# Two attentions inside one core's hybrid kernel: cycles of eight even units, mixed score phases, and another split of the query and key sums

## The reference

```python
x = x + attn_a(layernorm(x))   # heads of 8 -> latent 32, rope, q' = q_lat @ wqk.T + b, causal softmax over 256 keys
x = x + ffn(layernorm(x))      # logits = flat @ gate_w + gate_b, top 2 of 8 experts, gelu MLP 128 -> 512 -> 128
x = x + attn_b(layernorm(x))   # heads of 8, causal softmax(q k / sqrt(8)) v, out @ Wo.T + bo
x = x + ffn(layernorm(x))      # the same experts again
```

## Time and profile before

| | us |
|---|---|
| median of three runs | 1544.81 |
| the three runs | 1544.81, 1550.25, 1526.23 |
| the profiled execution | 1524.42 |
| its span, first to last instruction | 1520.8 |
| granted TensorE clock over the span | 0.818 |
| busy: TensorE, VectorE, ScalarE, GpSimd | 1175.3, 789.3, 655.4, 856.6 |

### The profile page before, as it was taken

The page is one execution under the profiler, slowest core; times in us unless marked ns, Lnnn a source line. Parts: engine busy times, 40 slices in busy tenths (PEclk is TensorE's granted clock), DMA queues, the critical chain, the costliest instruction groups (busy, mean ns, idle before and its releaser), DMA issues.

```text
span 1520.8 us, 31294 instructions
## 1 busy us (share of the span) xinstructions
PE 1175.3 (77%) x11163; PEld 907.0 (60%) x11164; DVE 789.3 (52%) x1878; ACT 655.4 (43%) x1214; POOL 856.6 (56%) x1173
## 2 busy tenths in 40 slices
PE   2699998989898889557999377888889837899600
PEld 2566666666666666447999244555556526899600
DVE  4555545454545544383554156666666647456322
ACT  0244445354444544203555344666667610455300
POOL 0456556565556654165552567887766518555276
PEclk8588869697978988657999677999999955999855
DMA  8000000000000000002223000000000000233222
GB/s 208 0 2 1 2 8 2 8 8 2 9 1 8 2 8 2 28 0 58 78 76 59 24 18 16 22 23 22 20 4 8 15 21 14 67 76 75 51 80 74
DMA packets 56245, 45.69 MB, mean 30 GB/s; under 512 B 13570, under 2 KB 48258, under 8 KB 56130
## 3 DMA queue, kind: packets, MB, share of 16 engines
q0 software_dynamic: 9088, 18.63, 5.6%
q1 hardware_dynamic: 39378, 22.44, 5.2%
q10 hardware_dynamic: 7664, 3.04, 0.9%
HBM read 27.57 MB, written 16.52 MB: 29 GB/s over the span
## 4 chain that ended last, share of the span: by engine, by line
PE 57%; DVE 15%; ACT 9%; POOL 7%; issue 6%; DMA 3%; another core or an unknown queue 1%; ACTq 1%; DVEq 1%; POOLq 0%
PE PS L1617 9%; PE PS L1331 5%; PE PS L1441 5%; POOL got L657 5%; PE PS L1333 4%; PE PS L1332 4%; PE PS L1382 4%; PE PS L1400 4%; ACT PT L1130 3%; PE PS L1429 3%; PE PS L1413 2%; DVE M L854 2%; PE PS L1426 2%; ACT xn L1116 2%; DMA b_cols<-in_L_ffn_b_dram 2%
## 5 line engine op out<-in xcount | busy, mean ns | idle before, releaser
L1130 ACT ACTIVATE PT<-PS 128x768 f32<-128x768 f32 x256 | 207.0, 809 | 307.0 <-PE PS L1451 224.7
L553 POOL TENSOR_SCALAR_AFFINE_SELECT PT<-PT 128x256 f32<-128x256 f32 x512 | 200.9, 416 | 202.0 <-ACT PT L1130 201.2
L853 DVE TENSOR_REDUCE M<-PS 128x4 f32<-128x512 f32 x128 | 88.7, 693 | 271.2 <-PE PS L1429 180.2
L686 POOL DMA_INDIRECT xg<-normed,source x156 | 150.0, 961 | 116.6 <-PE PS L1595 80.0
L657 POOL DMA_INDIRECT got<-expert_rows,slot_of x128 | 122.1, 954 | 80.6 <-DMA expert_rows<-y_rows 46.3
L1257 ACT ACTIVATE hid<-PS,b_cols 128x256 f32<-128x256 f32 x312 | 122.3, 475 | 96.4 <-PE PS L1333 74.4
L1617 PE MATMUL PS<-W,hid 128*128 x1248 | 156.1, 279 | 3.2 <-ACT hid L1257 2.7
L854 DVE TENSOR_REDUCE M<-PS 128x4 f32<-128x1024 f32 x128 | 155.6, 1216 | 0.0
L1617 PEld LDWEIGHTS PS<-W,hid 128*128 128x128 f32 x1248 | 149.4, 195 | 4.5 <-issue 4.5
L1382 PE MATMUL PS<-causal_b,ident_b 128*128 128x256 bf16 x512 | 112.0, 306 | 48.4 <-DVE q_aug L916 28.9
L1400 PE MATMUL PS<-PT,v_aug 128*32 128x256 f32 (+1 forms) x2048 | 124.8, 367 | 12.6 <-POOL PT L553 12.6
(11 more groups left out here) (263 smaller groups left out, 3061.7 us busy)
## 6 DMA issues: line engine op xcount, KB each, us to landing
expert_rows<-y_rows SPq DMA_DIRECT2D x78, 128.0 KB
normed<-xn SPq DMA_DIRECT2D x16, 256.0 KB, 2.3
xg<-normed,source POOLq DMA_INDIRECT x156
W<-in_L_ffn_w_dram SPq DMA_DIRECT2D x1, 2048.0 KB, 16.0
got<-expert_rows,slot_of POOLq DMA_INDIRECT x128, 2.5
out_dram<-X SPq DMA_DIRECT2D x8, 256.0 KB
b_rows<-in_L_ffn_b_dram SPq DMA_DIRECT2D x2, 512.0 KB, 3.7
X<-in_L_attn_a_x_dram ACTq DMA_DIRECT2D x2, 256.0 KB, 4.5
```

The source lines that it names most:

```text
L553: ins = nc.gpsimd.affine_select(out=diagonal, in_=diagonal, pattern=[[0, 2], [1, P]], compare_op=ALU.is_ge, fill=0.0, base=0, channel_mult ...
L686: nc.gpsimd.indirect_dma_start(out=xg[:, i % 4, b_, :], out_offset=None, in_=normed, in_offset=bass.IndirectOffsetOnAxis(ap=source[:, k:k ...
L1130: s.activation(PT[:, unit % 2, 2 * pair:2 * pair + 2, :], PS[:, 4:6, 0:3 * P], ACT.Exp).then_inc(m["exp_done"], 1)
```

## The change

In A the straight scores of the next unit and the turned scores of this one are issued together: `phase(unit, pair, unit + 1)` takes straight scores of two heads and turned scores of the other two, so four row bands are in use in each term, and there are two phases a unit. The maximum is taken in two halves (`pair_max`), one behind each phase. The lists are dealt out again: `second` (query2) in even units ahead of phase 0, `project` (a query or a key) between the phases in each unit, `close` (one step of another kind) after phase 1 in each unit. A chunk's gate comes one cycle later, normalizing is cut in halves or pairs of tiles, and the epilogue uses several banks.

In B the first scores stand behind prep, query 0 and key 0; the prologue has six steps instead of ten. Gathers and adds are one a unit after the first cycle, statistics are taken tile by tile, with buffers of their own for the gate. The query's sum is one VectorE operation from PSUM (bias and `minus` added, no `whole`), keys stay with GpSimd; `adds` places rows of the next chunk between the prologue's steps. SP's stores of the normalized chunks are written out instead of looped.

The core of the diff (deep indentation shortened by twelve):

```diff
@@ class Step, PlanA, Plan @@
     FIRST = [("prep", 0, 7), ("query", 0, 6), ("key", 0, 5), ("value", 0, 4), ("query", 1, 7), ("key", 1, 6), ("query2", 0, 5)]
-    LATE = [None, ("turn", 1, -1), None, ("prep", 0, 1), None, ("value", 0, 1), None, ("gate_t", 0, -1)]
-    EXTRA = [("gate", 0, -2), None, ("out_t", 0, -1), None, ("out", 0, -1), None, ("turn", 0, 0), None]
-    LAST = [("gate", 0, -1), ("turn", 1, 0), ("out_t", 0, 0), ("out", 0, 0), ("gate_t", 0, 0), ("gate", 0, 0)]
+    CLOSE = [("value", 0, 1), ("turn", 1, -1), ("gate_t", 0, -2), ("gate", 0, -2), ("out_t", 0, -1), ("out", 0, -1), ("prep", 0, 2), ("turn", 0, 0)]
+    FIRST_CLOSE = [None, None, ("prep", 0, 1), None, ("value", 0, 1), None, ("prep", 0, 2), ("turn", 0, 0)]
+    LAST = [("turn", 1, 0, 7), ("gate_t", 0, -1, 0), ("gate", 0, -1, 1), ("out_t", 0, 0, 2), ("out", 0, 0, 3), ("gate_t", 0, 0, 7), ("gate", 0, 0, 0)]
...
-    FIRST = [("prep", 0, 7), ("query", 0, 6), ("key", 0, 5), ("value", 0, 4), ("query", 1, 7), ("key", 1, 6),
- ("query", 2, 5), ("key", 2, 4), ("query", 3, 6), ("key", 3, 7)]
+    FIRST = [("prep", 0, 7), ("query", 0, 6), ("key", 0, 5), ("query", 1, 7), ("key", 1, 6), ("value", 0, 4)]
...
-    LATE = [("value", 0, 1), ("turn", 1, -1), ("out_t", 0, -1), ("out", 0, -1), ("prep", 0, 2), ("turn", 0, 0), ("gate_t", 0, -1), ("gate", 0, -1)]
+    LATE = [("turn", 0, -1), ("turn", 1, -1), ("value", 0, 1), ("gate_t", 0, -2), ("out_t", 0, -1), ("out", 0, -1), ("gate", 0, -2), ("prep", 0, 2)]
...
+    LAST = [("turn", 1, 0, 7), ("gate_t", 0, -1, 0), ("out_t", 0, 0, 1), ("gate", 0, -1, 2), ("out", 0, 0, 3), ("gate_t", 0, 0, 7), ("gate", 0, 0, 0)]
...
@@ gathers_at, adds_at @@
-    return (c + 3, range(2 * u - 4, 2 * u - 2)) if 2 <= u < 6 and c + 3 < NCH else None
+    return (c + 3, range(u, u + 1)) if c + 3 < NCH else None
...
+        return {0: (1, range(5, 8)), 2: (2, range(0, 4)), 4: (2, range(4, 8)), 6: (3, range(0, 4)), 7: (3, range(4, 6))}.get(u)
+    chunk, k = (c + 3, u - 2) if u >= 2 else (c + 2, u + 6)
+    return (chunk, range(k, k + 1)) if chunk < NCH else None
...
@@ GpSimd, attention_a and attention_b @@
-        early = plan.early[unit]
+        if unit and plan.project[unit - 1]:
+            end_rope(plan.project[unit - 1])
+        mask(m, unit, 0)
         if u % 2 == 0 and unit // 2 + 1 < NCH * G:
             key_low(unit // 2 + 1)
-        if early:
-            start_rope(early)
-        mask(m, unit, 0)
-        if early:
-            end_rope(early)
+        if plan.project[unit]:
+            start_rope(plan.project[unit])
         mask(m, unit, 1)
-        if unit + 1 < NCH * UNITS and normal_a(unit + 1):
...
+    def stack_keys(s):
+        pool.wait_ge(m["freed_act"], s.freed)
+        nc.gpsimd.tensor_tensor(ks[:, s.c % 2, s.g, :, :].rearrange("p b s -> p (b s)"), whole[:, 1, :],
+                                minus[:, 1, :].bitcast(F32), ALU.add).then_inc(m["keys_ready"], 1)
+    gather_results("1", 1, range(0, 3))
+    root(m, 1)
+    for s in plan.prologue:
+        if s.kind == "key":
+            stack_keys(s)
+    gather_results("1", 1, range(3, 2 * CT))
+    for unit in range(NCH * UNITS):
+        c, u = divmod(unit, UNITS)
+        if plan.early[unit] and plan.early[unit].kind == "key":
+            stack_keys(plan.early[unit])
+        mask(m, unit, 0)
+        if plan.late[unit] and plan.late[unit].kind == "key":
+            stack_keys(plan.late[unit])
+        mask(m, unit, 1)
+        if gathers_at(unit):
+            gather_results("1", *gathers_at(unit))
+        if root_at(unit):
+            root(m, *root_at(unit))
+        if u == 1:
...
@@ VectorE: closing, pair_max, attention_a, attention_b @@
+    elif s.kind == "query":
+        dve.wait_ge(m["queries_minus"], s.stacked)
+        v.scalar_tensor_tensor(qs[:, s.c % 2, s.g, :, :].rearrange("p b s -> p (b s)"), at, w["bias"][:, 0, s.g:s.g + 1],
+                               minus[:, 0, :].bitcast(F32), ALU.add, ALU.add).then_inc(m["freed_dve"], 1)
...
+def pair_max(m, unit, pair):
+    dve.wait_ge(m["s_ready"], 2 * unit + pair + 1)
+    banks, cols = slice(2 - 2 * pair, 4 - 2 * pair), slice((2 - 2 * pair) * L, (4 - 2 * pair) * L, L)
+    v.tensor_reduce(M[:, 0, cols], PS[:, banks, 0:P], AX, ALU.max, negate=True)
+    ins = v.tensor_reduce(M[:, 1, cols], PS[:, banks, P:3 * P], AX, ALU.max, negate=True)
+    if pair == 1:
+        ins.then_inc(m["max_ready"], 1)
...
-    row_max(m, 0, 0)
+    pair_max(m, 0, 0)
+    pair_max(m, 0, 1)
     for unit in range(NCH * UNITS):
         c, u = divmod(unit, UNITS)
         if unit + 1 < NCH * UNITS:
-            row_max(m, unit + 1, 0)
-        if plan.late[unit]:
-            closing(m, w, plan.late[unit], True)
-        if u % 2 == 0 and unit // 2 + 1 < NCH * G:
+            pair_max(m, unit + 1, 0)
+        if plan.second[unit]:
             query_low(unit // 2 + 1)
-        if plan.early[unit]:
-            swap(plan.early[unit])
-        if plan.extra[unit]:
-            closing(m, w, plan.extra[unit], True)
+        if unit + 1 < NCH * UNITS:
+            pair_max(m, unit + 1, 1)
+        if plan.close[unit]:
+            closing(m, w, plan.close[unit], True)
         if statistics_a(unit) is not None:
             if statistics_a(unit) < c:
                 dve.wait_ge(m["freed_dve"], plan.find("out", 0, c - 1).freed)
             statistics(m, statistics_a(unit))
+        if plan.project[unit]:
+            swap(plan.project[unit])
...
+    add_expert_rows("1", 1, range(0, 2), False)
+    adds = {("prep", 0): 2, ("query", 0): 3, ("key", 0): 4}
     for s in plan.prologue:
         closing(m, w, s, False)
-    row_max(m, 0, 3 * HD)
+        if (s.kind, s.g) in adds:
+            k = adds[s.kind, s.g]
+            add_expert_rows("1", 1, range(k, k + 1), False)
+        if (s.kind, s.g) == ("key", 0):
+            row_max(m, 0, 3 * HD)
     for unit in range(NCH * UNITS):
         c, u = divmod(unit, UNITS)
         join_max(unit)
+        if c and adds_at(unit):
+            chunk, rows = adds_at(unit)
+            add_expert_rows("1", chunk, rows, False)
+        if plan.early[unit]:
+            closing(m, w, plan.early[unit], False)
         if unit + 1 < NCH * UNITS:
             row_max(m, unit + 1, 3 * HD)
         if plan.late[unit]:
             closing(m, w, plan.late[unit], False)
-        if adds_at(unit):
-            add_expert_rows("1", *adds_at(unit))
-        if statistics_at(unit) is not None:
-            if statistics_at(unit) < c:
...
@@ ScalarE: attention_a, attention_b @@
-        if plan.early[unit]:
-            step(plan.early[unit])
+        if plan.second[unit]:
+            step(plan.second[unit])
+        exponent(m, unit, 0)
+        if plan.project[unit]:
+            step(plan.project[unit])
...
         exponent(m, unit, 1)
-        if plan.extra[unit]:
-            step(plan.extra[unit])
         if normal_a(unit):
...
-            s.activation(whole[:, which, :], at, ACT.Identity, bias=w["bias"][:, which, st.g:st.g + 1])
+            if which:
+                s.activation(whole[:, which, :], at, ACT.Identity, bias=w["bias"][:, which, st.g:st.g + 1])
...
@@ TensorE: attention_a, attention_b @@
+    def phase(unit, pair, next_unit):
+        turned, straight = [(2 * pair + h, 4 + h) for h in range(2)], [(2 - 2 * pair + h, 2 - 2 * pair + h) for h in range(2)]
+        rows = [slice(j * L, (j + 1) * L) for j in range(G)]
...
+        if ni is not None and pair == 0:
+            pe.wait_ge(m["queries_ready"], ni + 1)
+            pe.wait_ge(m["keys_ready"], ni + 1)
+        if unit >= 0 and unit + pair:
             pe.wait_ge(m["exp_done"], 2 * unit + pair)
...
+        for term, (q, k, kt, qt) in enumerate(((q_h, k_h, k_h, q_h), (q_l, k_h, k_l, q_h), (q_h, k_l, k_h, q_l))):
+            if ni is not None:
+                for j, at in straight:
+                    t_.matmul(bank[at][:, P:3 * P], q[rows[j], ni % 3, nb, P:S], k[rows[j], ni % 3, nb, :], start=False, stop=False, skip_group_check=True)
+            if unit >= 0:
+                for j, at in turned:
+                    t_.matmul(bank[at][:, 0:S], kt[rows[j], i3, b_, 0:P], qt[rows[j], i3, b_, :], start=(term == 0), stop=False, skip_group_check=True)
+            if ni is not None:
+                for j, at in straight:
+                    ins = t_.matmul(bank[at][:, 0:P], q[rows[j], ni % 3, nb, 0:P], k[rows[j], ni % 3, nb, 0:P], start=False, stop=(term == 2), skip_group_check=True)
+                if term == 2:
+                    ins.then_inc(m["s_ready"], 1)
+            if unit >= 0:
+                for j, at in turned:
+                    t_.matmul(bank[at][:, S:S + P], kt[rows[j], i3, b_, P:S], qt[rows[j], i3, b_, P:S], start=False, stop=False, skip_group_check=True)
+        if unit >= 0:
+            pe.wait_ge(m["mt_copied"], unit + 1)
...
-    scores(0)
+    phase(-1, 0, 0)
+    phase(-1, 1, 0)
     end = NCH * UNITS
     for unit in range(end):
         turn_max(m, unit)
```

(26 more changed lines are left out.)

293 lines of the change are left out of this document (133 added, 160 removed).

## The result

| | before | after |
|---|---|---|
| median, us (four runs each) | 1535.52 | 1325.74 |
| the runs | 1524.38 to 1550.25 | 1321.54 to 1335.02 |
| ratio, with its 95% interval | | 0.866 (0.858 to 0.874) |
| profiled execution, its span | 1524.42, 1520.8 | 1335.02, 1331.7 |
| granted TensorE clock over the span | 0.818 | 0.856 |

The direction was right and the size was not: 1390 was forecast with a range from 1350, and it is 1326. The windows of the changed kernel by stage (the columns of the earlier trace rows): attention A, its end, the bridge into B, attention B, its end.

What follows compares the result with a forecast made beforehand. The prediction took TensorE's work, waits and half clock to bound attention A; 1524.42 - 118 (attention A) + 4 (ends) - 4 (attention B's start) - 5 (its first cycle) - 12 (its middle) = 1389, said as 1390 us, range 1350 to 1455.

Steps and rivals of the forecast that it cites:

- TensorE's work: Attention A: TensorE's busy work per cycle of eight units falls from 55.3 to 48.1 us.
- 0.90 us of work a unit for mixing: Attention A: two mixed phases cost 2.14 us where separate scores cost 3.04, saving 7.2 us a cycle.
- The rival in which the kinds don't overlap: Attention A: straight and turned scores don't overlap, or new waits of that size: 56 us more, 1446 us; 12%.
- The waits and the half clock: Attention A: waits of 2.4 and 1.2 us, half clock 2.5, unseen 0.8; cycles of 55 us, -118 us together.
- the heap on VectorE in unit 6: Attention A: prep's closing, statistics and swap queued ahead of unit 8's half maxima make TensorE wait 1.2 us once a cycle.
- The ends: Ends of both attentions: the later gate adds mainly a copy and a transposition, +2 us each, +4 us.
- B's start: Start of attention B: first scores go out earlier, but additions waiting for gathers hold the first maximum; -4 us.
- My bound without that wait: Start of attention B: -11 us if the additions were not in the way of the first maximum.
- B's first cycle: Attention B: the first cycle goes from 54.95 to 50 us, -5 us, bounds -10 and +5.
- B's middle: Attention B, five cycles: moved query sums and spread gathers, adds and statistics leave 4.5 us waiting of 7; -12 us.
- The danger in the additions: Attention B: an add ahead of the maximum can lose a whole key sum, up to 1.29 us in 34 units, 44 us.
- the slow rival: Attention A: TensorE granted half clock throughout, cycles of 82 us, +80 us instead of -118, 1587 us; 4%.

Runs made afterwards that it cites:

- kernel 1: The changed kernel with mixing undone in attention A (scores of all four heads first, maximum taken once), new step lists kept: 1390.07 us, ratio 0.911.
- kernel 5: The changed kernel with one extra VectorE maximum in unit 3 of every cycle of attention A but the first, longer each cycle: 1380.74 us, one run.
- kernel 2: The kernel before with only the mixed phases and the two half maxima put in, its step lists untouched: 1502.56 us, ratio 0.985.
- kernel 3: The changed kernel with attention A's query and key projections back at the unit's head on TensorE and ScalarE: 1397.14 us, ratio 0.916.
- kernel 4: The changed kernel with the next unit's maximum taken in one piece behind the second phase: 1347.75 us, ratio 0.880.
- kernel 11: The changed kernel with the last five gathers before attention B issued ahead of the first key sum on GpSimd: 1319.47 us, ratio 0.858.
- kernel 10: The changed kernel with the root ahead of the unit's gathers on GpSimd in attention B: 1322.63 us, ratio 0.858.
- kernel 9: The changed kernel with attention B's gathers and additions back in bursts, the statistics following the additions: 1346.67 us, ratio 0.876.
- kernel 8: The changed kernel with attention B's query sums back on GpSimd: 1328.35 us, ratio 0.863.
- kernel 6: The changed kernel with a small extra VectorE maximum in every unit of attention A after the first cycle, growing each cycle: 1337.55 us, one run.
- kernel 7: The changed kernel with a small extra GpSimd sum in every unit of attention A after the first cycle, growing each cycle: 1352.28 us, one run.

## Why the prediction was wrong, point by point

**TensorE's work: right, in part by luck.** 48.1 us a cycle forecast, 47.4 busy in 47.7 measured. A phase takes its 1.07 us. But the step under the sum, 0.90 us of work a unit for mixing, measured 0.77, and only a wait of 0.13 that the unmixed order has brings it to 0.90 (7.16 by eight, kernel 1). And the unmixed new order is busy for 53.6 us where the sum began from 55.3. The two misses, 1.1 and 1.7, nearly cancel. The rival in which the kinds don't overlap is out: the Trainium skill's rule ("TensorE: Matmul & The Clock Gate", Part 3) on concurrent row groups holds in this trace for the mixture too, with starts 0.01 us apart.

**The waits and the half clock: the step that failed.** I charged 0.3 us a unit for the maximum and the exponents, 1.2 for the heap on VectorE in unit 6, 2.5 for half a stretch of half clock and 0.8 for the unseen: 6.9 us a cycle, where 0.3 came. By 7.8 cycles that is 51 us, A's whole miss, and the sum's own bound for A, cycles of 52 us and 140 less, was passed as well (167.9). The small waits were the worst chain taken against TensorE's time and charged to every unit: in the forecast VectorE's second half maximum was up to 0.3 us late, in the trace it ends 0.57 us early (271.64, asked for at 272.21) and 0.47 to 1.28 early in seven of the cycle's eight units, and kernel 5 measures 1.2 us of room in a unit with a closing step. The heap of unit 6 did come, much smaller. VectorE works without a pause from 301.97 until the maximum is ready at 307.36; 6.8 us behind the phase (which ends at 300.53), not 7.9, while TensorE could ask at 6.7, as forecast. It waits 0.20 us:

```profile
307.41 0.44 PE L1440 MATMUL PS<-C,M 128*128 128x128 f32 x2 [0.20 <-DVE M L867]
```

With no wait over 0.32 us between 95 and 410 us there was no half clock to pay, so the 2.5 us hung wholly on the 1.2 before it. I had named the right link between the two and then charged both ends of it, each a little, in place of saying that they stand or fall together: either 3.6 us of waits and the clock's price on top, or neither.

**How it divides.** My account credited mixing with 7.2 us a cycle and the order with the rest, 9.6. The order alone is worth 16.9, mixing alone 3.6, the two 24.1 (kernels 1 and 2). With the mixing in place the order is worth 20.5 (68.26 to 47.74), and of these 9.0 hang on the projection's place (kernel 3). The halves of the maximum, 1.9 (kernel 4), belong to the mixing: kernel 2 has them and kernel 1 does not. Which of the order's other moves carry the remainder I did not separate.

**The ends.** +4 forecast, -0.8 and +1.2 measured (B's end before, to its last logit: 22.8 us; after, 24.0). Small, and too high in A.

**B's start: right, with its mechanism.** 3.8 of 4 us, and the first scores 14.8 us sooner in the bridge where some 14 were forecast. The first scores did go out 10 us ahead of the first maximum (694.0 and 704.2), which stood behind additions waiting for gathers. My bound without that wait, 11 us, was 10.2 in kernel 11 (3.8 + 6.4); its limit is a step that I had in the chain only as work, the value's closing.

**B's first cycle: wrong in sign.** 5 less forecast, 6 more measured, one beyond the bound. I counted GpSimd's work there and the additions that leave, and did not follow the queue: the root now stands behind two gathers, ScalarE behind the root, the exponents behind ScalarE. The rule that I had written for VectorE, to name what is queued behind a waiting instruction, was not applied to ScalarE. Kernel 10 gets 4.4 of the 6 back, 2.4 of them in unit 2; what else the cycle lost is open, and profiles of the same code differ there by 3.4 us.

**B's middle: right in sign, half the size.** 12 forecast, 24.8 measured, at the edge of the bound. The 12 stood for the sums that leave GpSimd and for the spread together, undivided. Of the two the spread of gathers and additions brought something (kernel 9: 3.8 us in the fourth cycle, 12 in B, about half of the gain), and the sums on VectorE cost 0.7 a cycle (kernel 8); the other half of the gain is not assigned. Here I had the correct fact in hand: the loop through the sum and the maximum, 5.0 us, "just hidden". The short units show it, 4.24 us where kernel 8 has 3.81.

**The rivals.** The danger in the additions came about only in small. One line, L1135 in B, durations min, median and max:

```profile
L1135 DVE SCALAR_TENSOR_TENSOR X<-got,weight,X x51: 333/353/1455, 713.3 to 928.5; 128x128 f32<-128x128 f32 x51
```

The median is what it was in the earlier trace rows. Two additions took over 1 us, and both met a key sum; one of them, timeline:

```profile
744.29 1.28 POOL L616 TENSOR_TENSOR ks<-whole,minus 128x512 fp32r<-128x512 f32 x1 [0.41 <-ACT minus L1262]
744.64 1.08 DVE L1135 SCALAR_TENSOR_TENSOR X<-got,weight,X 128x128 f32<-128x128 f32 x1 [0.31 <-DMA got<-expert_rows,slot_of]
```

It ends 0.15 us behind the sum, and so does the other; a third, which had begun 0.30 us before its key sum did, took 0.345 us. By the Trainium skill's rule ("SBUF — State Buffer", section "SBUF: two separate sides") they could each have lost a key sum's time, and the trace agrees with the rule: the one that comes second waits. Twenty more took 0.40 to 0.59 us, and each ends 0.14 us behind a mask. All 51 together lost 4.6 us against 0.35 each, and from the second cycle on none met a key sum. The prediction's "lone long add" was a misreading of a row that shows only the longest: before, five took over 1 us, each beside a sum on GpSimd, and together they lost 10.2. None of the rivals, all slower than the forecast, came; I had none on the fast side, and so the range's low end of 1350 was only the sum's own bound. In the slow rival a sum is off: cycles of 82 instead of 55 are 211 us more in A, some +92 and not +80, and 1600.

## What to carry to other kernels

Where TensorE waits in a few long pieces, price the waits and the half clock behind them as one item that comes or goes whole, and give the case that it goes a chance of its own. Ask of each step where it stands against the two queues that it passes: the same step one phase later was worth as much as the better matmul order. And when work is moved between engines and at the same time spread out, measure the two apart, for the gain may lie in the spreading while the move costs.

## What the runs showed of the hardware

- Thirteen waits of 0.5 to 0.8 us in a cycle of 56.75 us left TensorE's clock at 1.00 in three cycles of six, and cost a stretch of 3 us at half clock in the others (kernel 3). Single waits of 1.09 and 2.16 us were followed by about 4 us at half, one of 1.33 by 7, waits of 3.2 to 4.4 by 12 (kernel 5, the profile after). But six of 1.05 to 1.39 us in kernel 6 and one of 1.48 in kernel 7 were followed by none.
- The same wait of 1.33 us in the same code lowered the clock in three profiles of eight, and a wait of 1.46 us did not. What tells these apart stayed open; so did why the clock first rises at 69 us in one run and at 84 in another.
- A maximum over 256 more elements of SBUF costs VectorE 0.267 us (0.408 to 2.010 us for 256 to 1792 elements, kernel 6). A sum of two inputs on GpSimd costs 0.108 us for 64 more elements (0.283 us for 64, 0.933 for 448, the shortest of each size in kernel 7).
- A VectorE operation with two inputs in SBUF and a sum on GpSimd did not run side by side: the sums of 192 and 256 elements that began during VectorE's product in `swap` took some 0.46 us more than the others (kernel 7), and two additions that met a key sum lasted until 0.15 us behind its end, 1.08 and 1.46 us instead of 0.35 (the profile after).
